# First group's maxima written into the score stack by ScalarE, third group projected at unit 7

## The reference

```python
x = x + attention(layernorm(x))          # causal, 16 heads, q, k and v of 32 numbers a head, then @ Wo
x = x + head_attention(layernorm(x), ctx) # per token: 16 heads of x against 16 heads of ctx, causal over heads
x = x + ffn(layernorm(x))                # one 256x256 matrix rounded to int4 steps, a bias, a rank-16 term
```

## Time and profile before

| | |
|---|---|
| time, median of 3 runs | 806.22 us (806.05 to 807.44) |
| the profiled execution's own time | 807.63 us |
| its span | 805.8 us |
| mean granted TensorE clock | 0.975 of full speed |
| busy: PE / PEld / DVE / ACT / POOL | 93 / 66 / 75 / 50 / 61 % of the span |
| chain that ended last, by engine | PE 62 %, DVE 15 %, DMA 12 %, issue 4 %, ACT 3 %, POOL 3 % |
| in that chain, DMA stack_k<-k_lo | 10 % |
| in that chain, DMA stack_q<-max_row | 1 % |

### The profile page before, as it was taken

How to read it: one execution, slowest core, us unless ns; L and a number is a source line. 1 busy time by engine, 2 the same in 40 slices (tenths; PEclk the granted TensorE clock), 3 DMA queues, 4 the chain that set the end, 5 groups by cost and what they waited for, 6 DMA issues and landing times.

```text
span 805.8 us, 16218 instructions
## 1 busy us (share of the span) xinstructions
PE 746.7 (93%) x5733; PEld 529.4 (66%) x5733; DVE 603.2 (75%) x1227; ACT 403.6 (50%) x760; POOL 493.2 (61%) x458
## 2 busy tenths in 40 slices
PE   8779899998999999999999999999999998889996
PEld 6656565765675656667666667576757674469996
DVE  3454555456686987698879987998698968699984
ACT  5114555554664557375736564756465545642111
POOL 5000000020876888598868887888878895986753
PEclk9979999999999999999999999999999998999999
DMA  5976666857784676577756775777567760100101
GB/s 186 127 94 106 81 80 86 138 77 90 92 131 70 93 96 86 99 98 116 96 98 89 114 96 95 99 115 98 82 87 113 100 98 8 60 8 14 34 14 39
DMA packets 47981, 70.55 MB, mean 88 GB/s; under 512 B 4897, under 2 KB 22578, under 8 KB 47922
## 3 DMA queue, kind: packets, MB, share of 16 engines
q1 hardware_dynamic: 46898, 69.52, 57.7%
q10 hardware_dynamic: 1024, 0.26, 0.2%
HBM read 14.98 MB, written 4.19 MB: 24 GB/s over the span
## 4 chain that ended last, share of the span: by engine, by line
PE 62%; DVE 15%; DMA 12%; issue 4%; ACT 3%; POOL 3%; SPq 1%; DVEq 0%; ACTq 0%; POOLq 0%
PE misc L542 22%; PE exp_bank L542 14%; DMA stack_k<-k_lo 10%; PE max_bank L542 10%; PE acc_bank L542 8%; PE sum_bank L542 7%; DVE head_out L1263 3%; DVE neg_max L1251 2%; DVE ln_raw L1229 2%; DMA stack_q<-max_row 1%; ACT x_in L932 1%; POOL prod L325 1%; DVE prod L370 1%; PE misc L592 1%; ACT probs L972 1%
## 5 line engine op out<-in xcount | busy, mean ns | idle before, releaser
L972 ACT ACTIVATE probs<-exp_bank 128x512 f32<-128x512 f32 x320 | 188.4, 594 | 172.5 <-PE exp_bank L542 101.5
L1251 DVE TENSOR_REDUCE neg_max<-max_bank 128x1 f32<-128x512 f32 (+1 forms) x192 | 129.2, 681 | 110.9 <-PE max_bank L542 110.3
L1633 POOL TENSOR_TENSOR prod<-head_probs,ctx_sb 128x256 f32<-128x256 f32 (+1 forms) x100 | 181.7, 1850 | 2.2 <-POOL head_probs L1628 0.5
L542 PE MATMUL max_bank<-stack_k,stack_q 96*128 96x384 f32 (+3 forms) x512 | 155.6, 366 | 24.0 <-DVE neg_max L1251 12.8
L542 PE MATMUL exp_bank<-stack_q,stack_k 97*128 97x384 f32 (+3 forms) x512 | 148.6, 352 | 14.5 <-ACT probs L972 10.8
L325 POOL TENSOR_TENSOR prod<-x1n,ctx_sb 128x256 f32<-128x256 f32 (+1 forms) x104 | 158.5, 1555 | 3.7 <-ACT x1n L932 3.7
L542 PE MATMUL acc_bank<-probs,values 128*32 128x512 f32 (+3 forms) x1024 | 152.7, 457 | 0.0
L542 PE MATMUL sum_bank<-probs,ones 128*32 128x512 f32 (+3 forms) x1024 | 150.5, 455 | 0.0
L1567 POOL TENSOR_TENSOR ln_var<-ln_mv,eps 128x4 f32<-128x4 f32 x21 | 4.4, 212 | 195.9 <-DVE ln_mv L1237 195.9
L1251 DVE TENSOR_REDUCE seg_max<-max_bank 128x4 f32<-128x512 f32 x128 | 86.6, 685 | 36.9 <-PE max_bank L542 35.6
L542 PEld LDWEIGHTS exp_bank<-stack_q,stack_k 97*128 97x128 f32 x512 | 84.0, 193 | 43.7 <-ACT probs L972 31.8
(11 more groups left out here) (186 smaller groups left out, 1392.6 us busy)
## 6 DMA issues: line engine op xcount, KB each, us to landing
stack_q<-q_hi SPq DMA_DIRECT2D x62, 256.0 KB, 5.6
stack_k<-k_hi SPq DMA_DIRECT2D x62, 256.0 KB, 9.3
stack_q<-q_lo SPq DMA_DIRECT2D x31, 256.0 KB, 6.9
stack_k<-k_lo SPq DMA_DIRECT2D x31, 256.0 KB, 10.5
x_in<-in_x SPq DMA_DIRECT2D x9, 512.0 KB, 5.6
ctx_sb<-in_ctx SPq DMA_DIRECT2D x32, 128.0 KB, 2.8
x<-in_x SPq DMA_DIRECT2D x7, 512.0 KB, 10.2
out<-y_sb SPq DMA_DIRECT2D x5, 512.0 KB, 3.2
```

What stands on the lines that cost most here:

```text
L542: return nc.tensor.matmul(*args, **kw)
L972: nc.scalar.activation(probs[:, (UNITS * g + n) % PTR, :], exp_bank[n % 2][:, :], ACT.Exp, scale=SCALE).then_inc(exp_done, 1)
L1251: vec.tensor_reduce(o, v, axis=AX_X, op=ALU.max, negate=True).then_inc(max_taken, 1)
L1633: last = gp.tensor_tensor(pv_prod[:, COFF[j]:COFF[j + 1]].rearrange("p (q d k) -> p q d k", q=4, k=keys), head_probs[:, 4 * j:4 * j + 4, N ...
```

## The change

For the first group of the first batch alone, the 128 x 16 maxima are turned one column at a time: 16 transposes, each with one column of `neg_max` as the weights, write a single row of 128 each on partition 0. The four heads go to four PSUM banks that are otherwise unused at that point (`exp_bank[0]`, `exp_bank[1]`, `sum_bank`, `misc[1]`), 512 values in each. ScalarE then copies each of these rows of 1 x 512 directly into row 96 of `stack_q`, with four copies. The copy to `max_row` and the DMA are gone for this group, and TensorE's wait at the start of pass (0, 0) is on ScalarE's semaphore `max_row_ready`. All later groups keep the transpose, the copy and the DMA.

The third group's projection, with its copies and subtractions, moves from unit 4 to unit 7 of `FIRST_PASS` on TensorE, ScalarE and VectorE.

```diff
         FIRST_PASS = (-1, 2)
-        THIRD_SPLIT = 4
+        THIRD_SPLIT = 7
+        first_row_banks = (exp_bank[0], exp_bank[1], sum_bank, misc[1])
...
+            def turn_first_maxima():
+                pe.wait_ge(max_ready, n_max_ready.up())
+                take(1, max_row_ready, r_row)
+                for h in range(G):
+                    for t in range(NT):
+                        last = nc.tensor.transpose(first_row_banks[h][0:1, t * P:(t + 1) * P],
+                                                   neg_max[:, 0, h, t:t + 1], ident[:, :])
+                last.then_inc(max_psum, 1)
...
-                    if st["C"]:
+                    if (i, g) == (0, 0):
+                        pe.wait_ge(max_row_ready, 1)
+                    elif st["C"]:
                         pe.wait_ge(max_stacked, n_row.up(16))
                     for n in range(UNITS):
                         if st["M"] and n == 1 and i < 0:
                             keep_busy(acc_bank, IDLE_ROW)
-                            turn_maxima(st["M"][1])
+                            turn_first_maxima()
...
-                        if st["M"] and n == 1:
+                        if (i, g) == (-1, 3) and n == 1:
+                            act.wait_ge(max_psum, n_row.up())
+                            for h in range(G):
+                                last = copy(stack_q[STACK:STACK + 1, 0, h, :], first_row_banks[h][0:1, :])
+                            last.then_inc(max_row_ready, 1)
+                        elif st["M"] and n == 1:
                             m_slot = st["M"][1]
                             act.wait_ge(max_psum, n_row.up())
                             wait(act, max_stacked, n_row_free.up(16) - 32)
```

## The result

The changed kernel's median is 801.24 us, against 807.44 us for the kernel before on the same chip: a ratio of 0.9924, with a 95 % interval of 0.9902 to 0.9946. One of the five launches of the changed kernel was slow (833.85 us at a mean granted clock of 0.848) and is left out of the ratio. Two later comparisons of the same two kernels, with 12 launches of the changed one and 24 and 29 of the one before, gave 0.9950 (0.9932 to 0.9967, median 801.94) and 0.9949 (0.9928 to 0.9971, median 802.23). The kernel is faster by 0.5 to 0.8 %, 4 to 6 us.

What follows compares the result with a forecast made beforehand. Bound: TensorE's wait for the first maxima's DMA, queued behind the third stack, and the clock lost with it. 807.63 - 6.2 (4.0 wait, 2.2 clock) = 801.4 us profiled, 1.4 less for the median: 800.0 us; range 798.4 to 803.2.

Steps and rivals of the forecast that it cites:

- The hole and its cause: TensorE stands still 52.87 to 56.69 us; the 8 KB maxima DMA lands only with the third stack, at 56.3.
- The copies: Four ScalarE copies of the maxima row after the turn: 2.0 us, 4.8 us to spare, so no cost.
- The turn: 16 one-column transposes for one on TensorE's path before group 1: 1.8 us in all, +1.7 us.
- The move: Third group's projection at unit 7 in pass (-1, 2): maxima ready at 44.1 us, -1.7 us.
- Pass (0, 0): Starts at about 52.6 us; group 2's first maxima at 57.4 instead of 63.67, a gain of 6.2 us.
- The late stack DMAs: Third group's moved stack DMAs still land near 56.3 us; rival with a gap: 58.3, total 800.9 us, chance 0.10.
- after that nothing: After group 2's first maxima the rest moves along: cost 0, with 1.5 us either way for the clock.
- The wait of 4.0 us: Part of the gain at group 2's first maxima from removing the DMA's wait: 4.0 us, 0.2 included.
- the clock's part of the sum: 2.2 us that the units and projection of pass (0, 0) lost at the low clock and would regain.
- my second rival: A low clock stretch in or after the turn takes about 3 us of the gain: 803.0 us, chance 0.17.
- The slower rival: Clock stays low from the turn through pass (-1, 3), transposes counting as idle: +1.3, 807.5 us, chance 0.04.

Runs made afterwards that it cites:

- The move alone: Kernel before with the third group projected at unit 7 instead of 4, the maxima's DMA kept: ratio 1.0009 to the kernel before.
- the row put first: Kernel before, but SyncE issues the third group's six stack DMAs only once the row of maxima has landed: ratio 1.0029 to the kernel before.
- the shorter version: Changed kernel with k's high part copied before the third exponential in pass (0, 0), 5 idle matmuls for 12 in pass (-1, 3): ratios to before 0.9906, 0.9910.
- Filling the hole: Kernel before with 34 or 20 idle matmuls put before TensorE's wait for the first row of maxima: ratios 1.0023 and 1.0013 to the kernel before.
- the fourfold turn: Changed kernel with each of the 16 one-column transposes done four times: 808.43 us, ratio 1.0024 to the kernel before.

## Why the prediction was right, and where it was off

**The hole and its cause** stood as written: 8 KB behind a third stack that lands at 56.3. The move alone and the row put first show it from both sides.

**The copies** were expected at 0.48 from start to start and 2.0 us in all, and took 47.21 + 0.57 - 45.76 = 2.02; they ended at 47.8, with 4.4 us to spare.

**The turn** was put at 1.8 us, and took 45.48 - 43.82 = 1.7.

**The move** was to bring the maxima at 44.1, and brought them at 43.76. I had the projection start at 36.75, and it started at 36.53.

**Pass (0, 0)** was to start at 52.6 and started at 52.18; group 2's first maxima were expected at 57.4 and came at 57.07. **The late stack DMAs** opened no gap: they land at 56.1 to 56.3 as before. That margin was thinner than I wrote, because ScalarE's copy of q waits for the same landing. In this pass that copy is not on the path, with the shorter version it is.

**The step that was off is "after that nothing", costed at 0 with 1.5 us either way.** The sum gave 800.0 us, and all three medians lie inside its range (801.24, 801.94, 802.23). But 6.2 us was worked out from one trace, and the first comparison, which gave just that (807.44 - 801.24), rests on four launches against five. The 12-launch comparisons show about 4.1 us (0.50 and 0.51 % of 806), and both of their intervals leave out 6.2. The first agreement was in part luck. Two mechanisms are seen in the runs.

First, in the kernel before, the DMA's landing is a fixed time that swallows low stretches in the first 50 us; in the changed kernel they pass through, 1.3 us in the second profile. The wait of 4.0 us is therefore worth less in a launch that meets one.

Second, the clock's part of the sum, 2.2 us. Filling the hole gave back 2.1 us in the stage and nothing at the end. The change itself did better: the mean clock rises from 0.9758 to 0.9800 and from 0.9753 to 0.9789. The first profile of before loses about 5 us of clock between 38 and 66 us (mean 0.82, against 1.00 in the first profile of the changed kernel), which is 0.006 of the span. As an estimate from these numbers, some 60 % of it is kept in the average launch, and the rest turns up elsewhere. So my second rival, that the wait goes and the clock is lost anyway, is borne out in part only, and at other places than after the turn.

Launches of equal mean clock give a rough split. At 0.981 the kernel before takes 803.9 us (11 launches) and the changed one 801.4 (7); at 0.979 it is 804.9 (7) and 802.8 (8): 2.0 to 2.5 us at the same clock. Among the 96 launches of the kernel before in these comparisons, 0.004 more clock goes with 2.2 us less time, and that is the rest. The clock's term is thus about what the sum had, and the wait's came out smaller. The split is not a clean one, since a low stretch in the first 50 us lowers the mean clock of both kernels and delays only the changed one.

**Open** is how much each mechanism takes in the average launch, and why the fillers leave the mean clock where it was, when the change itself raises it. No run tells that apart.

**The slower rival**, transposes that do not hold the clock, is out by the fourfold turn: 64 of them in a row, and the clock stayed at 1.00.

## What to carry to other kernels

A small DMA issued behind a backlog lands with the backlog: read its time to landing against the same DMA's median, and move a few hundred values by an engine that is idle anyway if its copies fit under other work. Where TensorE falls to its lower clock behind a stall, the clock that a change gives back in that stage need not be a gain at the end: filling the hole with idle matmuls gave none here, and taking the wait away gave part of it. Count it only when many launches show it. A fixed landing time also shields the work behind it from earlier delays, so a gain read from two traces can be too large when the landing goes away.

## What the runs showed that I had not expected

- Launches of one kernel differ by up to 8 us (803.59 to 811.84) with the granted clock's average, and the low stretches near 34 us (clock 0.50), seen in a profile of six of the kernels, were in neither profile of the kernel before. One profile doesn't show how the clock behaves.
- Moving the third projection removed a low stretch at 41 to 47 us (six profiles of six with unit 4, none of eight with unit 7), and with the DMA still there no gain from it is seen.
- A ScalarE copy of one partition of 512 values takes 0.57 us, 0.48 from start to start, as long as one of 128 partitions (0.59 and 0.48 in the earlier trace rows).
- 64 one-column float32 transposes in a row ran at 0.108 us each with the clock at 1.00 throughout.
